# Expert masks spread over the partitions by TensorE instead of through DRAM, in a decoder layer on one core

## The chip, the cores and the metric

One Trainium2 chip, one of its cores. The metric is the device time of one execution of the whole kernel in microseconds; lower is better. TensorE (PE) multiplies into PSUM, VectorE (DVE), ScalarE (ACT) and GpSimd (POOL) do the rest, SyncE (SP) issues every transfer.

## The reference

Four batches of 512 rows with 128 features, three residual blocks behind a layer norm each. The third is the one that the change is about:

```python
x = x + attn(layernorm(x), gamma)                # scores are minus squared distances of the rows
x = x + xattn(layernorm(x), ctx, ctx, ...)       # 16 heads of 8, 154 context rows, ALiBi slopes
# x = x + ffn(layernorm(x), ...), with h the normed rows:
logits = einsum('bsh,eh->bse', h, router_w) + router_b
_, top = top_k(softmax(logits), 2)
mask = one_hot(top, 8).sum(-2)                   # 1 for each of a row's two experts, else 0
out = einsum('bse,ehd,bsd->bsh', mask, expert_w, h) + einsum('bse,eh->bsh', mask, expert_b)
```

Every expert is computed for every row, with the rows that did not choose it set to zero.

## The kernel before, in words

Each engine has a list of steps (`ORDER`), walked strictly in that order; `walk` (L110) calls a step as `steps[name](b, k)`, with `b` the batch and `k` a part of it. Semaphores between steps do the rest, so an engine whose next step has to wait holds up all its later steps. Batches overlap: while PE and ACT do the cross attention of one batch, the self attention and the queries of a later one are woven in. `WARM` gives, for some steps, a number of idle matmuls (`warm`, L825, recorded at L828) that PE does ahead of the step's wait, into a bank that nobody needs; they keep PE busy.

PSUM has eight banks. `ST` (two) holds attention scores. `MX` (two) holds the score groups whose row maxima DVE takes; batch `b` fills it 22 times (two groups in each of eleven `maxima` steps), in turn into the two banks, and the semaphores `a_ps` and `maxed` count filled and reduced groups. `MX[0]` also takes the transposed maxima (`mT`). `YV` takes the values' products, the output projection (`wo`), the router's logits and the experts' sum. `YM` takes transposes of `pvs`, `ao`, `y3`, of the masks and of the result `fT`. `A0` and `A1` serve the self attention and the queries.

What a batch passes through, with the lines used below:

- Self attention (`dist`, `soft`, `probs`, `self`), then `y2T` and `query`. DVE's `query` (L725 to L729) splits the queries into three bf16 parts; SP writes the parts to `q_scratch` and reads them back stacked into `qs`, which the maxima's matmuls (L928) need.
- `maxima` (PE L928, DVE L736), `mcat`, `mT`; SP carries `mT` through `m_scratch` into `qs`.
- `scores` (PE L952 and L957, exponentials ACT L584) in twelve parts, and `values` (PE L974 and L976), a part for each quarter of the heads. `values` of a batch's first part waits for `fT_sb`, as the experts of the batch before sat in the same bank `YV`.
- `divide` (transposes of `pvs`, DVE L757 and L759), `aoT`, `wo` (L996), third layer norm `y3`, its transpose `y3T`.
- `route`: PE L1009 multiplies `y3T` with the router's weights, DVE ranks the logits in seven instructions (L782 to L797) and leaves a bf16 mask. `mask`: PE transposes it (L833), ACT copies it to `maskT16`, whose first eight partitions are the eight experts' rows of 512 ones and zeros.
- The row of an expert has to lie on all 128 partitions before it can be multiplied with `y3T`. SP's `mask` writes the eight rows to `e_scratch` in DRAM and, when these have landed, reads them back in two transfers that repeat each row over 128 partitions, into `mask_all`.
- `select`: DVE (L807, experts 0, 2, 4, 6) and POOL (L504, experts 1, 3, 5, 7) multiply `mask_all` with `y3T` into `ym`, one instruction of 128x512 for each expert. Step `select` is one item of the list of either engine, so its four instructions are not parted.
- `experts` (PE): one bias matmul (L1025) and eight fp32 matmuls (L1028, two recorded instructions each), adding up in `YV`. It is one item of PE's list too.
- `fT` (ACT copy, PE transposes), `store` (DVE L813 adds the residual, SP stores).

In PE's list `experts:0` stands ahead of `dist:3`, `experts:1` ahead of `values:2.0`, `experts:2` ahead of `values:3.0`, and `experts:3` is last but one.

Of the kernel before, what the change touches and what calls it, by code (L numbers as in the profile page):

```python
# [15 lines left out]
E = 8
P = 128
# [42 lines left out]
        soft:3.1 scores:1.7 scores:1.8 scores:1.9 scores:1.10 scores:1.11 probs:3.0 values:1.1 soft:3.2  # L60
        values:1.3 soft:3.3 aoT:1 probs:3.1 probs:3.2 probs:3.3 mT:2 y3T:1 mask:1 scores:2.0 scores:2.1 y2T:3
        scores:2.2 scores:2.3 scores:2.4 scores:2.5 query:3 fT:1 scores:2.6 values:2.1 scores:2.7 scores:2.8
        scores:2.9 scores:2.10 scores:2.11 values:2.3 aoT:2 y3T:2 mT:3 mask:2 scores:3.0 scores:3.1 scores:3.2
        scores:3.3 scores:3.4 fT:2 scores:3.5 scores:3.6 scores:3.7 scores:3.8 scores:3.9 scores:3.10
# [7 lines left out]
        divide:0.1 maxima:1.9 maxima:1.10 mcat:1 wo:0 y3:0 gather:2 route:0 y2:2 y1:3 query:2 select:0 dist:3
        rowmax:3 maxima:2.0 maxima:2.1 maxima:2.2 maxima:2.3 maxima:2.4 maxima:2.5 maxima:2.6 maxima:2.7 store:0
        divide:1.0 divide:1.1 maxima:2.8 maxima:2.9 wo:1 maxima:2.10 mcat:2 y3:1 gather:3 route:1 y2:3 select:1
        query:3 store:1 divide:2.0 maxima:3.0 maxima:3.1 maxima:3.2 maxima:3.3 maxima:3.4 maxima:3.5 divide:2.1
        maxima:3.6 maxima:3.7 wo:2 maxima:3.8 y3:2 maxima:3.9 maxima:3.10 mcat:3 route:2 select:2 store:2
# [1030 lines left out]
```

## Time and profile before

| | us |
|---|---|
| median of 3 runs | 294.41 |
| lowest and highest | 293.37 to 298.64 |
| profiled execution, its device time | 294.32 |
| its span in the trace | 292.2 |
| mean granted TensorE clock, 1 is 2.4 GHz | 0.951 |
| busy: PE, PEld (weight loads) | 232.6, 111.6 |
| busy: DVE, ACT, POOL | 162.9, 109.3, 62.0 |

The span runs from the first to the last instruction of the profiled execution; some 2.1 us of the device time lie around it. Busy times overlap between engines. PE's busy time holds the warm matmuls, and as matmuls are pipelined, the mean length of one (393 ns for 512 columns of bf16) is more than its share of PE: back to back ones start closer together.

### The profile page before, as it was taken

To read this page: it belongs to the slowest core of one execution; us is meant where nothing else is said; L and a number is where in the kernel's file an instruction comes from. 1 tells how busy PE (TensorE), PEld (TensorE's weight loads), DVE (VectorE), ACT (ScalarE), POOL (GpSimd) and SP (SyncE) were. 2 spreads that over 40 slices of the span, in tenths; PEclk is the share of its full clock that TensorE was granted. 3 is DMA by queue.
4 is the path that set the end of the run, shared out by engine and by line. 5 is a ranking of instruction groups with operands and counts; after the bars stand their busy time and mean duration, and the time that the engine had idled before them with its cause. 6 is when DMAs were issued, how large, how long until landed. Compare 5 with 4: busy or idle time off the path is not lost.

```text
span 292.2 us, 3460 instructions
## 1 busy us (share of the span) xinstructions
PE 232.6 (80%) x1182; PEld 111.6 (38%) x1198; DVE 162.9 (56%) x406; ACT 109.3 (37%) x200; POOL 62.0 (21%) x112
## 2 busy tenths in 40 slices
PE   6778669777997899869997897978867698867774
PEld 2427323245332447434332752422334232143331
DVE  3856644993542887965673892915775240034270
ACT  2346055322774263570574318144102615210000
POOL 5234350001512001334000040800010260001071
PEclk9979999999798899999999999999979999789599
DMA  6942239002062012075001024170100600000231
GB/s 182 267 119 53 52 109 192 19 1 47 3 168 48 0 36 47 1 251 110 0 1 34 2 48 142 58 161 2 34 2 15 213 3 0 3 0 0 55 126 36
DMA packets 23029, 19.28 MB, mean 66 GB/s; under 512 B 10644, under 2 KB 21260, under 8 KB 22924
## 3 DMA queue, kind: packets, MB, share of 16 engines
q1 hardware_dynamic: 23012, 19.07, 25.2%
q8 instruction: 9, 0.15, 0.2%
q14 instruction: 8, 0.07, 0.1%
HBM read 13.65 MB, written 5.41 MB: 65 GB/s over the span
## 4 chain that ended last, share of the span: by engine, by line
PE 46%; DVE 26%; ACT 10%; issue 6%; DMA 6%; POOL 3%; another core or an unknown queue 1%; SPq 0%; ACTq 0%; DVEq 0%; POOLq 0%
DVE nm L736 10%; PE bank L1028 10%; PE bank L833 6%; PE bank L976 5%; PE bank L974 5%; ACT pt L584 4%; PE bank L868 4%; PE bank L828 3%; PE bank L928 3%; PE bank L887 2%; PE bank L952 2%; DMA qs<-m_scratch 2%; DVE st L628 2%; PE bank L996 2%; DMA mask_all<-e_scratch 2%
## 5 line engine op out<-in xcount | busy, mean ns | idle before, releaser
L736 DVE TENSOR_REDUCE nm<-bank 128x3 f32<-128x462 f32 x88 | 49.3, 619 | 18.8 <-PE bank L928 18.7
L584 ACT ACTIVATE pt<-bank 128x512 f32<-128x512 f32 x80 | 44.1, 596 | 31.6 <-PE bank L952 20.2
L828 PE MATMUL bank<-idle 128*128 128x512 bf16 x147 | 42.9, 434 | 3.1 <-DVE idle L623 1.5
L928 PE MATMUL bank<-kA,qs 128*128 128x308 bf16 (+1 forms) x172 | 29.9, 270 | 9.3 <-DVE nm L736 8.4
L428 POOL TENSOR_SCALAR ve<-mv 128x4 f32<-128x4 f32 x12 | 2.3, 194 | 155.9 <-DVE mv L631 155.7
L504 POOL TENSOR_TENSOR ym<-mask_all,y3T 128x512 f32<-128x512 bf16 x16 | 25.1, 1596 | 43.8 <-DMA mask_all<-e_scratch 43.8
L807 DVE TENSOR_TENSOR ym<-mask_all,y3T 128x512 f32<-128x512 bf16 x16 | 22.6, 1469 | 20.6 <-DMA mask_all<-e_scratch 20.6
L1028 PE MATMUL bank<-ym,ewT 128*128 128x512 f32 x64 | 28.7, 601 | 1.7 <-DVE ym L807 1.7
L952 PE MATMUL bank<-qs,kB 128*128 128x512 bf16 x58 | 20.4, 393 | 9.6 <-ACT pt L584 6.8
L828 PEld LDWEIGHTS bank<-idle 128*128 128x128 bf16 x154 | 16.5, 111 | 23.6 <-issue 11.2
L928 PEld LDWEIGHTS bank<-kA,qs 128*128 128x128 bf16 x172 | 13.0, 100 | 28.4 <-DVE nm L736 21.9
L974 PE MATMUL bank<-pt,vm 128*32 128x512 f32 x128 | 17.9, 632 | 7.1 <-ACT pvs L514 5.0
L868 PE MATMUL bank<-y1Tg,y1T 128*128 128x512 f32 x32 | 17.8, 639 | 4.6 <-ACT w L530 3.8
L655 DVE TENSOR_REDUCE rm<-bank 128x1 f32<-128x512 f32 x16 | 11.0, 691 | 18.4 <-PE bank L869 15.2
L976 PE MATMUL bank<-pt,vt 128*128 128x512 f32 x32 | 19.3, 687 | 0.0
L1028 PEld LDWEIGHTS bank<-ym,ewT 128*128 128x128 f32 x64 | 11.7, 189 | 17.0 <-issue 6.6
L530 ACT ACTIVATE w<-bank,snsq,sgn 128x512 f32<-128x512 f32 x16 | 12.3, 777 | 15.3 <-DVE rm L655 15.3
L887 PE MATMUL bank<-y,pT 128*128 128x128 f32 x128 | 15.2, 277 | 0.0
L514 ACT ACTIVATE fT<-bank 128x512 f32<-128x512 f32 x4 | 2.4, 597 | 34.0 <-PE bank L1028 34.0
L952 PEld LDWEIGHTS bank<-qs,kB 128*128 128x128 bf16 x64 | 6.2, 100 | 22.8 <-ACT pt L584 16.7
L887 PEld LDWEIGHTS bank<-y,pT 128*128 128x128 f32 x128 | 14.6, 192 | 0.2
L638 DVE TENSOR_SCALAR y<-x,mv,rs 128x128 f32<-128x128 f32 x32 | 10.3, 382 | 6.4 <-POOL rs L430 6.4
(132 smaller groups left out, 281.2 us busy)
## 6 DMA issues: line engine op xcount, KB each, us to landing
mask_all<-e_scratch SPq DMA_DIRECT2D x8, 512.0 KB, 4.8
qs<-q_scratch SPq DMA_DIRECT2D x8, 384.0 KB, 5.3
q_scratch<-qpart SPq DMA_DIRECT2D x4, 384.0 KB, 2.5
xs<-in_x_dram SPq DMA_DIRECT2D x4, 256.0 KB, 7.1
q_scratch<-qpart SPq DMA_DIRECT2D x4, 256.0 KB, 2.2
out_dram<-ob SPq DMA_DIRECT2D x4, 256.0 KB, 5.7
kA<-k_scratch SPq DMA_DIRECT2D x8, 120.0 KB, 2.8
kB<-k_scratch SPq DMA_DIRECT2D x8, 120.0 KB, 2.5
```

The source lines that it names most:

```text
L504: g.tensor_tensor(ym[:, e, :], mask_all[:, e, :], y3T[:, :], ALU.mult).then_inc(masked_p, 1)
L584: nc.scalar.activation(pt[:, n % PT_RING, :], ST[n % 2][:, :], ACT.Exp).then_inc(exps, 1)
L736: v.tensor_reduce(negated[:, GROUP * g:GROUP * g + heads], MX[n % 2][:, 0:heads * J].rearrange("p (s j) -> p s j", s=heads), AX.X, ALU.max ...
L807: v.tensor_tensor(ym[:, e, :], mask_all[:, e, :], y3T[:, :], ALU.mult).then_inc(masked_v, 1)
L828: mm(bank_[:, :], idle[:, 0:P], idle[:, :], start=True, stop=True)
L868: mm((A0, A1)[t % 2][:, :], y1T[:, tile(t)], y1Tg[:, :], start=True, stop=False)
L887: last = mm(A0[:, tile(t)], pT[:, t, u, :], y1[:, u, :], start=(u == 0), stop=(u == T - 1))
L928: last = mm(MX[n % 2][:, at * J:(at + heads) * J], qs[:, b % 2, a, tile(t)], kA[:, s:s + heads, a, 0:J], start=True, stop=True)
L952: last = mm(ST[n % 2][:, :], kB[:, h % 2, h // 2, 0:JM], qs[:, b % 2, h // 2, :], start=True, stop=True)
L974: mm(YV[32 * g:32 * g + 32, :], vm[:, b, R * g + k, :], pt[:, (n + g) % PT_RING, :], start=(k % 2 == 0), stop=False, skip_group_check=True)
L976: mm(YV[:, :], vt[:, b, k, :], pt[:, (n + G) % PT_RING, :], start=False, stop=(k % 2 == 1), skip_group_check=True).then_inc(pv_ps, 1)
L1028: last = mm(YV[:, :], ewT[:, e, :], ym[:, e, :], start=False, stop=(e == E - 1))
```

## The change

The masks' round trip through DRAM goes, with SP's step `mask`, `e_scratch`, `mask_all` and their semaphores. A constant `spread` (128 partitions x 8 x 128, bf16, loaded at the start, ahead of the experts' weights) holds for expert `e` a matrix whose row `e` is ones. A new PE step `spread:b.e` multiplies it with `maskT16` into a bank of `MX`: the expert's row on all partitions. DVE's `select:b.e` multiplies that bank with `y3T`; POOL's `select` is gone. `MX` is now filled by maxima and spreads in one common count (`mx_full`, `mx_free`), in this order of batches: maxima 0, maxima 1, spread 0, maxima 2, spread 1, maxima 3, spread 2, spread 3. `experts` and `select` are parted by expert, and each may stand anywhere in the lists. The experts' sum and the logits move from `YV` to `YM`, so `values` no longer waits for `fT_sb`. All five lists and `WARM` are new; of the lists the diff shows first three places of DVE's, then PE's around the masks of the four batches (what stood there before is told above).

```diff
-        keys:0 gather:0 y2:0 stats1:1 y1:1 query:0 dist:1 rowmax:1
+        keys:0 stats1:1 gather:0 y2:0 y1:1 query:0 dist:1 rowmax:1
...
-        wo:0 y3:0 gather:2 route:0 y2:2 y1:3 query:2 select:0 dist:3
+        wo:0 stats1:3 y3:0 gather:2 route:0 y2:2 select:0.0 select:0.1 y1:3
+        select:0.2 select:0.3 query:2 select:0.4 select:0.5 select:0.6 select:0.7 dist:3 maxima:2.0
...
-        maxima:2.10 mcat:2 y3:1 gather:3 route:1 y2:3 select:1
-        query:3 store:1 divide:2.0 maxima:3.0
+        maxima:2.10 mcat:2 y3:1 gather:3 route:1 y2:3 select:1.0 select:1.1
+        select:1.2 select:1.3 select:1.4 select:1.5 query:3 select:1.6 select:1.7 maxima:3.0
...
+        scores:1.1 scores:1.2 scores:1.3 values:1.0 mask:0 y2T:2 scores:1.4 spread:0.0 spread:0.1 query:2
+        experts:0.0 spread:0.2 spread:0.3 experts:0.1 spread:0.4 experts:0.2 experts:0.3 scores:1.5 spread:0.5
+        y1T:3 experts:0.4 experts:0.5 scores:1.6 spread:0.6 spread:0.7 dist:3 maxima:2.0 experts:0.6 scores:1.7
+        maxima:2.1 experts:0.7
...
+        route:1 scores:2.0 mask:1 scores:2.1 spread:1.0 spread:1.1 y2T:3 experts:1.0 spread:1.2 query:3
+        spread:1.3 spread:1.4 experts:1.1 spread:1.5 experts:1.2 experts:1.3 experts:1.4 scores:2.2 spread:1.6
+        experts:1.5 spread:1.7 scores:2.3 experts:1.6 scores:2.4 scores:2.5 values:2.0 scores:2.6 values:2.1
+        scores:2.7 maxima:3.0 experts:1.7 scores:2.8 maxima:3.1 scores:2.9 maxima:3.2 scores:2.10 fT:1
+        maxima:3.3 scores:2.11 values:2.2 maxima:3.4 values:2.3 maxima:3.5 divide:2.0
...
+        mT:3 route:2 mask:2 scores:3.0 spread:2.0
+        spread:2.1 scores:3.1 spread:2.2 spread:2.3 scores:3.2 experts:2.0 experts:2.1 scores:3.3 experts:2.2
+        spread:2.4 scores:3.4 experts:2.3 spread:2.5 scores:3.5 values:3.0 scores:3.6 experts:2.4 spread:2.6
+        scores:3.7 experts:2.5 scores:3.8 values:3.1 scores:3.9 spread:2.7 experts:2.6 scores:3.10 experts:2.7
+        scores:3.11 values:3.2 values:3.3 fT:2 divide:3.0 divide:3.1 aoT:3 wo:3 y3T:3 route:3 mask:3 spread:3.0
+        spread:3.1 experts:3.0 spread:3.2 experts:3.1 spread:3.3 spread:3.4 experts:3.2 spread:3.5 experts:3.3
+        experts:3.4 spread:3.6 spread:3.7 experts:3.5 experts:3.6 experts:3.7 fT:3
...
 WARM = {
-    "y1T:0": 16, "probs:0": 12, "y2T:0": 16, "query:0": 4, "y1T:1": 5, "maxima:0": 13, "scores:0": 3, "y2T:1": 1,
-    "divide:0.0": 1, "y3T:0": 2, "mask:0": 8, "y2T:2": 3, "route:1": 3, "mask:1": 11, "scores:2": 1, "y3T:2": 5,
-    "route:2": 1, "mask:2": 5, "scores:3": 9, "experts:2": 1, "wo:3": 1, "y3T:3": 13, "mask:3": 4,
-    "experts:3": 14, "fT:3": 2,
+    "y1T:0": 16, "probs:0": 10, "y2T:0": 16, "query:0": 4, "y1T:1": 4, "maxima:0": 14, "scores:0": 7, "y2T:1": 1,
+    "query:1": 2, "values:0.0": 2, "maxima:1": 1, "scores:1": 2, "y3T:1": 3, "scores:2": 6, "spread:1": 1,
+    "wo:2": 1, "y3T:2": 3, "scores:3": 1, "wo:3": 3, "y3T:3": 16, "mask:3": 7, "spread:3": 1,
 }
...
+        def maxima_fill(b, g):
+            return b * GROUPS + E * max(0, b - 1) + g
+        def spread_fill(b, e):
+            return min(b + 2, B) * GROUPS + E * b + e
...
+            load(spread[:, :, :], spread_rows, expert_in)
             load(ewT[:, :, :], expert_w, expert_in)
...
-            def mask(b, _):
-                sp.wait_ge(mask_sb, b + 1)
-                load(e_scratch, maskT16[0:E, :], e_out)
...
-                for i in range(2):
-                    half = slice(i * E // 2, (i + 1) * E // 2)
-                    load(mask_all[:, half, :], e_scratch[half, :].partition_broadcast(P), e_in[i])
...
-                    pe.wait_ge(fT_sb, b)
+                    pe.wait_ge(x2_ready, b)
...
+            def select(b, e):
+                if e == 0:
+                    dve.wait_ge(y3T_sb, b + 1)
+                    if b >= 1:
+                        dve.wait_ge(f_ps, b)
+                n = spread_fill(b, e)
+                dve.wait_ge(mx_full, n + 1)
+                v.tensor_tensor(ym[:, e, :], MX[n % 2][:, :], y3T[:, :], ALU.mult).then_inc(mx_free, 1)
...
+            def spread_(b, e):
+                n = spread_fill(b, e)
+                if e == 0:
+                    pe.wait_ge(mT_sb, min(b + 2, B))
+                    pe.wait_ge(mx_free, n)
+                    warm(MX[n % 2], f"spread:{b}")
+                    pe.wait_ge(mask_sb, b + 1)
...
+                pe.wait_ge(mx_free, n - 1)
+                mm(MX[n % 2][:, :], spread[:, e, :], maskT16[:, :], start=True, stop=True).then_inc(mx_full, 1)
+            def experts(b, e):
+                if e == 0:
+                    pe.wait_ge(mask_sb, b + 1)
...
+                    mm(YM[:, :], ebias[:, :], maskT16[:, :], start=True, stop=False)
+                pe.wait_ge(mx_free, spread_fill(b, e) + 1)
+                last = mm(YM[:, :], ewT[:, e, :], ym[:, e, :], start=False, stop=(e == E - 1))
+                if e == E - 1:
+                    last.then_inc(f_ps, 1)
```

## Rows read from the trace of the kernel before

**Rows 1.** The page's slices: granted TensorE clock in tenths, 40 slices of 7.3 us.
```profile
PEclk9979999999798899999999999999979999789599
```

**Rows 2.** Stretches: us, busy us of PE, PEld, DVE, ACT, POOL, clock, DMA share, GB/s.
```profile
0.00:117.09 117.09, 92.80 (x518) 48.00 (x525) 72.88 (x211) 50.49 (x93) 28.27 (x84) 0.96 0.35 84
...
117.09:137.39 20.30, 16.54 (x72) 7.86 (x74) 14.52 (x30) 9.48 (x17) 8.36 (x7) 1.00 0.48 130
...
170.93:200.57 29.64, 25.05 (x111) 9.93 (x111) 15.00 (x31) 12.06 (x22) 8.99 (x7) 1.00 0.35 93
...
200.57:226.84 26.27, 19.79 (x116) 10.04 (x117) 19.02 (x48) 5.75 (x10) 1.21 (x2) 0.94 0.06 14
...
226.84:255.84 29.00, 24.12 (x92) 7.56 (x95) 6.09 (x5) 11.93 (x22) 6.38 (x4) 0.94 0.17 55
...
272.06:292.20 20.14, 14.62 (x40) 5.91 (x41) 6.08 (x5) 1.19 (x2) 6.37 (x4) 0.84 0.27 79
```

**Rows 3.** The same stretches, warm matmuls (L828) alone: PE and PEld busy, clock, DMA.
```profile
117.09:137.39 20.30, 2.71 (x11) 0.95 (x11) 1.00 0.48 130
...
200.57:226.84 26.27, 5.65 (x19) 2.03 (x20) 0.94 0.06 14
```

**Rows 4.** Groups by form: busy us, mean ns; idle before, releaser.
```profile
L1028 PE MATMUL bank<-ym,ewT 128*128 128x512 f32 x64 | 28.7, 601 | 1.7 <-DVE ym L807 1.7
...
L504 POOL TENSOR_TENSOR ym<-mask_all,y3T 128x512 f32<-128x512 bf16 x16 | 25.1, 1596 | 43.8 <-DMA mask_all<-e_scratch 43.8
...
L807 DVE TENSOR_TENSOR ym<-mask_all,y3T 128x512 f32<-128x512 bf16 x16 | 22.6, 1469 | 20.6 <-DMA mask_all<-e_scratch 20.6
...
L813 DVE TENSOR_TENSOR ob<-bank,x 128x512 f32<-128x512 f32 x4 | 2.8, 689 | 18.5 <-PE bank L833 18.5
```

**Rows 5.** Waits of the maxima's matmuls: us in total, times, longest.
```profile
PE bank L928 <- DVE nm L736: 8.4, 31, 2.2
```

**Rows 6.** Chain that ended last, last batch from the masks' copy: start, us, what.
```profile
272.71 0.61 ACT maskT L514
...
273.33 1.30 DMA e_scratch<-maskT
...
274.71 4.47 DMA mask_all<-e_scratch
...
279.30 0.70 DVE ym L807
...
280.05 7.30 PE bank L1028 x16
...
287.38 0.60 ACT fT L514
```

**Rows 7.** Timeline, batch 1's masks to batch 3's first maxima: start, us, what, idle.
```profile
175.64 0.40 PE L833 MATMUL bank<-ident,maskp 128*128 128x128 bf16 x4 [0.63 <-DVE maskp L797]
...
192.25 0.85 SPq L311 DMA_DIRECT2D qs<-q_scratch  x2
...
200.57 0.56 PE L928 MATMUL bank<-kA,qs 128*128 128x308 bf16 x4
```

**Rows 8.** Timeline, first values matmuls at two clocks and their successors.
```profile
191.00 1.07 PE L974 MATMUL bank<-pt,vm 128*32 128x512 f32 x8 [0.69 <-ACT fT L514]
...
193.06 1.06 PE L974 MATMUL bank<-pt,vm 128*32 128x512 f32 x8
...
250.23 1.94 PE L974 MATMUL bank<-pt,vm 128*32 128x512 f32 x8 [1.19 <-ACT pvs L514]
```

**Rows 9.** Timeline, early: POOL before two norms, warm matmuls back to back.
```profile
32.82 0.20 POOL L428 TENSOR_SCALAR ve<-mv 128x4 f32<-128x4 f32 x1 [7.12 <-DVE mv L631]
...
37.34 0.19 POOL L428 TENSOR_SCALAR ve<-mv 128x4 f32<-128x4 f32 x1 [2.14 <-DVE mv L631]
...
48.56 2.97 PE L828 MATMUL bank<-idle 128*128 128x512 bf16 x13
```

**Rows 10.** The page's DMA issues: KB each, median us from issue to landing.
```profile
qs<-q_scratch SPq DMA_DIRECT2D x8, 384.0 KB, 5.3
```

More of the change, by code:

```diff
@@ L56 @@
+        query:0 y1T:1 dist:1 soft:1.0 soft:1.1 probs:1.0 soft:1.2 soft:1.3 probs:1.1 probs:1.2 probs:1.3 mT:0
         scores:0.0 scores:0.1 scores:0.2 scores:0.3 y2T:1 scores:0.4 query:1 scores:0.5 scores:0.6 y1T:2
-        scores:0.7 scores:0.8 dist:2 values:0.1 soft:2.0 scores:0.9 scores:0.10 scores:0.11 soft:2.1 soft:2.2
-        values:0.3 probs:2.0 soft:2.3 aoT:0 probs:2.1 probs:2.2 probs:2.3 mT:1 y3T:0 scores:1.0 scores:1.1
-        scores:1.2 mask:0 y2T:2 query:2 scores:1.3 scores:1.4 scores:1.5 y1T:3 fT:0 dist:3 scores:1.6 soft:3.0
@@ L60 @@
[L60 to L64, printed above, removed]
@@ L65 @@
-        scores:3.11 values:3.1 values:3.3 aoT:3 y3T:3 mask:3 fT:3
+        scores:0.7 scores:0.8 values:0.1 dist:2 soft:2.0 soft:2.1 soft:2.2 scores:0.9 scores:0.10 soft:2.3
+        scores:0.11 probs:2.0 probs:2.1 values:0.3 probs:2.2 probs:2.3 aoT:0 mT:1 y3T:0 scores:1.0 scores:1.1
+        scores:1.2 scores:1.3 mask:0 y2T:2 scores:1.4 query:2 scores:1.5 y1T:3 scores:1.6 dist:3 scores:1.7
+        scores:1.8 fT:0 soft:3.0 scores:1.9 scores:1.10 scores:1.11 soft:3.1 values:1.1 values:1.3 probs:3.0
@@ L66 @@
     """,
     "vector": """
-        stats1:0 y1:0 weights:0 dist:0 rowmax:0 keys:0 gather:0 y2:0 stats1:1 y1:1 query:0 dist:1 rowmax:1
+        stats1:0 y1:0 weights:0 dist:0 rowmax:0 keys:0 stats1:1 gather:0 y2:0 y1:1 query:0 dist:1 rowmax:1
         maxima:0.0 maxima:0.1 maxima:0.2 maxima:0.3 maxima:0.4 maxima:0.5 maxima:0.6 maxima:0.7 maxima:0.8
-        maxima:0.9 maxima:0.10 mcat:0 stats1:2 gather:1 y2:1 y1:2 query:1 stats1:3 dist:2 rowmax:2 maxima:1.0
-        maxima:1.1 maxima:1.2 maxima:1.3 maxima:1.4 maxima:1.5 maxima:1.6 maxima:1.7 divide:0.0 maxima:1.8
@@ L72 @@
[L72 to L76, printed above, removed]
@@ L77 @@
-        divide:3.0 divide:3.1 wo:3 y3:3 route:3 select:3 store:3
+        maxima:0.9 maxima:0.10 mcat:0 gather:1 y2:1 stats1:2 y1:2 query:1 dist:2 divide:0.0 rowmax:2 maxima:1.0
+        maxima:1.1 maxima:1.2 maxima:1.3 maxima:1.4 maxima:1.5 maxima:1.6 maxima:1.7 maxima:1.8 divide:0.1
+        maxima:1.9 maxima:1.10 mcat:1 wo:0 stats1:3 y3:0 gather:2 route:0 y2:2 select:0.0 select:0.1 y1:3
+        select:0.2 select:0.3 query:2 select:0.4 select:0.5 select:0.6 select:0.7 dist:3 maxima:2.0 maxima:2.1
@@ L83 @@
         scores:0.3 y2T:1 scores:0.4 query:1 scores:0.5 values:0.0 scores:0.6 y1T:2 scores:0.7 values:0.1
-        scores:0.8 dist:2 values:0.2 maxima:1.0 divide:0.0 maxima:1.1 scores:0.9 maxima:1.2 maxima:1.3
-        maxima:1.4 scores:0.10 maxima:1.5 probs:2.0 maxima:1.6 scores:0.11 maxima:1.7 values:0.3 maxima:1.8
-        probs:2.1 divide:0.1 probs:2.2 maxima:1.9 aoT:0 maxima:1.10 wo:0 probs:2.3 mT:1 self:2 y3T:0 scores:1.0
-        route:0 scores:1.1 scores:1.2 mask:0 y2T:2 query:2 scores:1.3 scores:1.4 y1T:3 scores:1.5 scores:1.6
@@ L88 @@
-        experts:0 dist:3 maxima:2.0 values:1.0 maxima:2.1 fT:0 scores:1.7 maxima:2.2 values:1.1 maxima:2.3
-        probs:3.0 scores:1.8 maxima:2.4 scores:1.9 maxima:2.5 scores:1.10 maxima:2.6 scores:1.11 values:1.2
-        maxima:2.7 values:1.3 divide:1.0 maxima:2.8 divide:1.1 probs:3.1 aoT:1 probs:3.2 maxima:2.9 wo:1
-        maxima:2.10 probs:3.3 self:3 mT:2 y3T:1 route:1 mask:1 scores:2.0 scores:2.1 y2T:3 scores:2.2 scores:2.3
-        scores:2.4 scores:2.5 query:3 scores:2.6 experts:1 values:2.0 values:2.1 scores:2.7 fT:1 divide:2.0
@@ L93 @@
[L93 to L97 removed]
+        scores:0.8 dist:2 divide:0.0 maxima:1.0 values:0.2 maxima:1.1 scores:0.9 maxima:1.2 maxima:1.3 probs:2.0
```

134 lines of the change are left out of this document (59 added, 75 removed).

## The prediction, made before the change was run

> **What bounds the kernel now.** I read the page's slices first, then busy time by stretch, the groups by form, the chain of waits, and the timeline where it led. No engine is full. The span is 292.2 us. PE comes nearest, but in the stretches from 117.09 on part of its time is warm matmuls: 2.71 of 16.54 us in the first and 5.65 of 19.79 us in the one from 200.57 [rows 2, 3]. So PE does real work in 13.8 of 20.3 us there, and in 14.1 of 26.3 us in the other. What fills the rest is order: PE's list is strict, and each batch comes to a point where masks must be spread before PE can go on. In the last batch nothing lies beside this. The masks are copied at 273.32, the first product starts only at 279.30, PE's expert block runs from 280.05 to 287.35, and the copy of the result starts at 287.38 [rows 6]: 14.06 us from masks to result copy, 5.98 of them transfers. In the other batches DVE and POOL wait for the same transfers (20.6 us over three waits on DVE, 43.8 on POOL [rows 4]). The clock bounds too: it is full in most slices, but 0.5 in the 38th [rows 1], and 0.84 to 0.94 in the late stretches [rows 2].
>
> **The change part by part.** Prices first.
>
> A product on DVE takes 0.70 us where it runs alone (the last batch's first, [rows 6]); over all 16 it is 1469 ns, and POOL's are 1596 ns [rows 4], because the two slow each other. The new one reads a PSUM bank and an SBUF tile as 128x512 fp32; the nearest row is the residual addition, 689 ns [rows 4]. I take 0.70. DVE then does eight in 5.6 us where it did four in 5.9 and POOL four in 6.4. Bounds: 0.69, and 1.47 if something still slowed them.
>
> A spread is a bf16 matmul of 512 columns, the form of a warm one: 13 take 2.97 us [rows 9]; with 0.38 us for the last to come through that is 0.216 apiece at full clock. 32 of them add 6.9 us of PE time. The expert block keeps its 7.30 us for 16 passes [rows 6], 0.91 an expert. The `WARM` tables hold 154 matmuls before and 121 after; 33 fewer are 7.1 us of filler, worth nothing by themselves as they sat in waits.
>
> *Tail (batch 3).* Masks ready at 273.32. First spread through at about 273.75, first product done at 274.45, first expert matmul at 274.5. Two spreads and the bias lie ahead of it; six more spreads lie inside. From there PE is the bound (0.91 + 0.22 an expert against 0.70 on DVE): 274.5 + 7.30 + 6 x 0.216 = 283.1, against 287.35: 4.25 us less. Before, 14 warm matmuls covered the wait for the transfers, and the 38th slice has the clock at half [rows 1]; now experts run in that time. Work worth 1.7 us less would be done if the half clock stayed to 277.6, where that slice ends (half of 274.1 to 277.6). I take half of that: **-3.4**, bounds -2.5 and -4.25.
>
> *Batch 2's masks (226.84 to 255.84, 29.00 us).* PE's real work here at full clock: 16 score matmuls 3.5, four tails at one such each 0.9, four `values` at 2.06 (start to start, [rows 8]) 8.2, experts 7.3, bias 0.2, spreads 1.7, transposes of `fT` 0.4 (fp32 columns at an expert's rate): 22.3. Before it was 20.5 in 29.0: scores and exponentials first, then the expert block in one piece while ACT stood still, then `values` at half clock once (1.94 us against 1.07 for the same eight [rows 8]). Now single experts lie between scores, so PE works while ACT does exponentials. ACT needs 11.9 [rows 2] and is no bound; the last exponentials and the copy of `pvs` stay exposed. I allow 2.2 of idle: 24.5, **-4.5**. Bounds: 0, and -6.7 with none.
>
> *Batch 1's masks to batch 3's maxima.* From the masks' transposes (175.64) to the first maxima of batch 3 (200.57) pass 24.9 us [rows 7]. Batch 3's queries came from DVE only behind its four slow products, so `qs` was asked for at 192.25, and PE had the expert block to finish. New order: scores 2.6, two `values` 4.1, seven experts and bias 6.6, spreads 1.7, `y2T` and `query` 1.3, masks 0.2: 16.6, and some 1.5 of waits give 18.1. The queries now stand behind six products. Masks copied by about 177.3, then on PE six spreads 1.3, two experts 1.8, `y2T` and `query` 1.3 and a wait or two: the sixth product ends near 183. Splitting the queries and writing them out I put at 4.4 (an estimate: three DVE instructions of at most 0.70 each, and a write no longer than half the 5.3 us of the read), so the request goes out near 187.4 and, at 5.3 us to landing [rows 10], is there by 192.7, in time for 193.7. That is 6.8 less. But one expert, `values` 2.2, a divide, transposes and a score part (4.3 us of PE) stood ahead of these maxima and now stand among them. DVE has 19.0 us to do in the 26.3 that follow and PE 14.1 [rows 2, 3], so I let half of it come back, with the spread work 2.3: **-4.5**, bounds 0 and -6.8.
>
> *Batch 0's masks (117.09 to 137.39, 20.3 us).* PE's real work was 13.8. It gains spreads 1.7 and `values:1.0` 2.06, and loses two experts, 1.8: 15.8. With 1.5 of waits it is 17.3: **-3.0**. The later work balances (a `values` less, two experts more). Bounds 0 and -4.5.
>
> *Start.* `stats1:1` moves ahead of `gather:0`, into DVE's idle time. POOL began that norm at 37.34 and had begun the one before at 32.82 [rows 9]; it can follow at 35.2, 2.1 earlier. Behind it come `y1T:1` and `dist:1`, but then maxima wait for `qs`, whose transfer doesn't move. I take **-1.0**, bounds 0 and -2.1. The extra load of 256 KB stands ahead of the experts' weights, for which POOL waits; POOL is then idle for 7.12 us before 32.82 [rows 9], which hides it. It would show only beyond that. SP loses its mask step, twelve transfers in all, so `query` is no longer behind a mask step; nothing is added there.
>
> The logits and experts in `YM`: `divide` waited for `YM` to be stored already, so this costs nothing, while `values` is freed from the experts. The remaining warm and order edits I set at nothing, within the bounds. The experts' new waits on DVE are the risk; they are the second and fourth rivals.
>
> Sum: 3.4 + 4.5 + 4.5 + 3.0 + 1.0 = 16.4. The profiled execution took 294.32 us (2.1 around its span), so 277.9; its time is 0.09 below the median of the runs, so **278.0 us**.
>
> A page speaks against this change. The Trainium skill, "TensorE: Matmul & The Clock Gate", section "A second HAM failure mode: psum-queue depth-cycling", tells of a kernel that went round PSUM banks, with small gaps on PE between groups of matmuls, and whose clock kept dropping and recovering. The trace agrees only in part: the maxima cycle through the same two banks with 31 waits of 0.27 us [rows 5], and most slices that hold them stand at 9 tenths [rows 1]. By the page the first rival below would come true; by the rows it is the lesser case.
>
> **The rivals.**
>
> *The clock falls in each expert block.* Spreads and experts alternate over two banks with gaps, and 33 warm matmuls are gone. For: `values` at half clock at 250.23, behind a stretch in which PE waited on exponentials; ahead of `scores:3` one warm matmul stands where nine did. Against: the new blocks are denser. There the eight matmuls took 1.94 for 1.07; a whole `values` part of 2.06 loses 1.7 at that ratio, and I take that for a fall. Four are 6.7 us, of which 0.9 is in my tail: 294.4 - 16.4 + 5.8 = **283.8**.
>
> *Hand-offs.* PE waits for DVE before each expert as it does in the maxima, 8.4 / 31 = 0.27 us [rows 5]; 32 x 0.27 = 8.7, hence **286.7**. Against it: two banks let a spread run ahead, and a product is shorter than an expert.
>
> *Only the exposed ends gain.* The middle batches are held by maxima, exponentials and the queries' transfers, and PE's freed time there turns into waiting. Then 3.4 + 4.5 = 7.9 remain: **286.5**. For it: 19.0 us of DVE work in 26.3 [rows 2].
>
> *Slower.* The experts go one at a time: spread, product, expert, with the next spread not issued until the expert is through, because in strict lists DVE's product stands behind work that waits for PE (`select:0.4` behind `query:2`). Idle of PE for each is then a product and both hand-overs, 0.70 + 0.27 + 0.1 = 1.07, or 34 us in all: **312**. It decides from 16.4 / 32 = 0.51 us of PE idle ahead of each expert. Against it: 31 waits in the maxima averaged half of that, over the same two banks and engines.
>
> *Everything at its good bound.* 4.25 + 6.7 + 6.8 + 4.5 + 2.1 = 24.4: **270.0**.
>
> **How the numbers follow.** Forecast 0.50, clock 0.13, hand-offs 0.12, only ends 0.09, slower 0.05, all good 0.11. A measurement of this kernel can tell about 2% from no change, so the limits are 288.5 and 300.3. The forecast's own spread (half of the distance to each bound) is 272 to 284; the range must take in the three rivals near 284 to 287 and the good case, but can leave the slower one out: **268 to 288**. Faster: all but the slower case and some of the upper ends of the middle three, 0.88; within 2% 0.07; slower 0.05.
>
> **What would show it.** Right: the first product of batch 3 starts within 0.6 us of the end of the masks' copy; products average 0.70; PE's idle ahead of L1028's successors stays under 0.1 us an expert; the last expert block takes 8.6 us or, at half clock, up to 10.3; the first maxima of batch 3 start 9 to 12 us earlier than at 200.57; from the first scores of batch 3 to its divide 24.5 us. Wrong: products at 1.4 us; a wait of PE on DVE's products of 0.5 us or more each; a mean clock under 0.9; the maxima of batch 3 as late as now; or queries of batch 2 or 3 that land later, since the middle of the sum hangs on them.

## The result, and the profile after

The changed kernel takes 279.66 us (median of 4 runs, 278.62 to 282.18) beside 296.52 us for the kernel before on the same chip (293.37 to 299.08): a ratio of 0.953, 95% interval 0.942 to 0.964. The forecast was 278.0 us. Executions of one kernel differ here by 1 to 3% with the clock they are granted, so differences of a few us are read from several kernels, and the ratios here and below (a kernel's time over that of the kernel before on the same chip) compare only the runs within 1.5% of their kernel's fastest.

The page's slices of the changed kernel (slices of 6.9 us), which answer [rows 1]:

```profile
PEclk9979979999999999999999999999997799979599
```

The 5 still stands in the 38th slice. Stretches between ACT's copies that end each batch's maxima (`mT:0` to `mT:3`), then to the last masks' copy, then to the end of the last result's copy (columns as in [rows 2]). The kernel before:

```profile
65.31:111.87 46.56, 39.97 (x218) 19.48 (x221) 27.40 (x76) 24.76 (x47) 8.67 (x25) 0.93 0.20 47
111.87:170.10 58.23, 49.94 (x292) 27.52 (x294) 39.59 (x98) 26.68 (x50) 10.79 (x11) 1.00 0.23 59
170.10:222.03 51.93, 42.00 (x212) 19.20 (x217) 32.93 (x79) 17.22 (x31) 10.20 (x9) 0.97 0.23 60
222.03:272.71 50.68, 38.36 (x164) 15.47 (x167) 15.02 (x35) 14.91 (x28) 7.58 (x6) 0.91 0.10 34
272.71:287.98 15.27, 13.32 (x32) 4.94 (x31) 5.39 (x4) 1.19 (x2) 6.37 (x4) 0.84 0.29 86
```

The changed kernel:

```profile
67.11:109.87 42.76, 38.68 (x227) 18.83 (x227) 26.35 (x68) 24.92 (x46) 6.43 (x14) 1.00 0.21 52
109.87:163.71 53.84, 48.53 (x293) 27.66 (x294) 38.69 (x109) 26.64 (x49) 8.22 (x18) 1.00 0.17 41
163.71:212.47 48.76, 39.81 (x209) 18.18 (x208) 31.74 (x81) 17.31 (x31) 3.87 (x5) 0.97 0.23 56
212.47:261.44 48.97, 39.78 (x177) 18.00 (x177) 15.43 (x40) 15.03 (x28) 1.20 (x2) 0.88 0.03 8
261.44:272.65 11.21, 10.28 (x26) 3.77 (x25) 5.25 (x8) 1.19 (x2) 0.00 (x0) 0.91 0.00 0
```

`mT:0` comes 1.8 us later (67.11 against 65.31). Then the stretches are 3.8, 4.4, 3.2, 1.7 and 4.1 us shorter: 17.1 in all, 15.3 net, against spans of 292.2 and 276.9. PE's busy time falls by 6.5 us (183.6 to 177.1 over these five), its idle time by 10.6 (39.1 to 28.5). The first 3.8 lie ahead of any mask: batch 0's masks are copied only in the second stretch.

Groups by form, which answer [rows 4]:

```profile
L1033 PE MATMUL bank<-ym,ewT 128*128 128x512 f32 x64 | 31.6, 596 | 0.0
L802 DVE TENSOR_TENSOR ym<-bank,y3T 128x512 f32<-128x512 f32 x32 | 21.1, 688 | 25.6 <-PE bank L1023 25.5
...
L1023 PE MATMUL bank<-maskT,spread 128*128 128x512 bf16 x32 | 11.6, 412 | 0.5 <-ACT maskT L510 0.3 <-DVE ym L802 0.2
```

The 32 products average 0.69 us, and the experts' matmuls have no idle time ahead of them. The tail's timeline, which answers [rows 6]:

```profile
261.44 0.60 ACT L510 ACTIVATE maskT<-bank 128x512 bf16<-128x512 bf16 x1 [5.14 <-PE bank L828]
262.09 1.04 PE L1023 MATMUL bank<-maskT,spread 128*128 128x512 bf16 x2 [0.26 <-ACT maskT L510]
262.84 1.29 DVE L802 TENSOR_TENSOR ym<-bank,y3T 128x512 f32<-128x512 f32 x2 [2.22 <-PE bank L1023]
263.58 1.13 PE L1033 MATMUL bank<-ym,ewT 128*128 128x512 f32 x2
...
272.05 0.60 ACT L510 ACTIVATE fT<-bank 128x512 f32<-128x512 f32 x1 [10.01 <-PE bank L1033]
```

From the masks' copy to the first product 0.80 us pass where 5.98 did (copy's end to product's start in both), to the result's copy 10.0 where 14.06 did. Batch 1's masks to batch 3's maxima, which answers [rows 7]:

```profile
169.63 0.40 PE L828 MATMUL bank<-ident,maskp 128*128 128x128 bf16 x4 [0.22 <-DVE maskp L791]
...
180.68 0.83 SPq L325 DMA_DIRECT2D qs<-q_scratch  x2
...
187.40 0.56 PE L923 MATMUL bank<-kA,qs 128*128 128x308 bf16 x4
...
187.79 0.64 DVE L730 TENSOR_REDUCE nm<-bank 128x3 f32<-128x462 f32 x1 [6.93 <-PE bank L923]
```

17.8 us where 24.9 passed. DVE now waits 6.93 us for these maxima: PE, no longer DVE's products and the queries, decides there.

### The profile page after: what moved, and what is told of

It is laid out like the page before. It is cut to its first block, busy times and chain, and to the rows that moved or that the text cites. A ratio compares the mean times of both kernels' runs of the same rounds, so it can differ in the third digit from the quotient of the medians.

```text
span 276.9 us, 3461 instructions
## 1 busy us (share of the span) xinstructions
PE 228.8 (83%) x1197; PEld 112.0 (40%) x1197; DVE 159.5 (58%) x422; ACT 109.5 (40%) x200; POOL 37.4 (13%) x96
## 4 chain that ended last, share of the span: by engine, by line
PE 59%; DVE 24%; ACT 6%; issue 6%; POOL 2%; DMA 1%; POOLq 0%; SPq 0%; DVEq 0%; ACTq 0%
PE bank L1033 10%; DVE nm L730 10%; PE bank L828 6%; PE bank L971 6%; PE bank L969 6%; PE bank L823 5%; PE bank L863 4%; PE bank L947 4%; PE bank L882 4%; PE bank L923 3%; PE bank L1023 3%; DVE y L632 2%; PE bank L1002 2%; ACT w L534 2%; PE bank L895 2%
## 5 line engine op out<-in xcount | busy, mean ns | idle before, releaser
L823 PE MATMUL bank<-idle 128*128 128x512 bf16 x121 | 36.5, 444 | 2.4 <-DVE idle L617 1.5
L802 DVE TENSOR_TENSOR ym<-bank,y3T 128x512 f32<-128x512 f32 x32 | 21.1, 688 | 25.6 <-PE bank L1023 25.5
L923 PE MATMUL bank<-kA,qs 128*128 128x308 bf16 (+1 forms) x172 | 28.5, 264 | 8.1 <-DVE nm L730 7.4
L1033 PE MATMUL bank<-ym,ewT 128*128 128x512 f32 x64 | 31.6, 596 | 0.0
L969 PE MATMUL bank<-pt,vm 128*32 128x512 f32 x128 | 16.9, 602 | 4.8 <-ACT pvs L510 4.8
L823 PEld LDWEIGHTS bank<-idle 128*128 128x128 bf16 x121 | 13.0, 112 | 19.2 <-issue 9.0
L649 DVE TENSOR_REDUCE rm<-bank 128x1 f32<-128x512 f32 x16 | 11.0, 691 | 16.8 <-PE bank L864 16.7
L971 PE MATMUL bank<-pt,vt 128*128 128x512 f32 x32 | 18.0, 645 | 0.0
L882 PE MATMUL bank<-y,pT 128*128 128x128 f32 x128 | 15.3, 278 | 0.0
L1033 PEld LDWEIGHTS bank<-ym,ewT 128*128 128x128 f32 x64 | 11.7, 190 | 7.5 <-DVE ym L802 3.7
L510 ACT ACTIVATE pT<-bank 128x512 f32<-128x512 f32 x16 | 9.1, 594 | 12.2 <-PE bank L828 12.2
L632 DVE TENSOR_SCALAR y<-x,mv,rs 128x128 f32<-128x128 f32 x32 | 10.3, 382 | 4.8 <-POOL rs L434 4.8
L534 ACT ACTIVATE w<-w,nrb,sgn 128x512 f32<-128x512 f32 x16 | 12.9, 805 | 0.3 <-DVE nrb L661 0.3
L434 POOL TENSOR_TENSOR rs<-ve,minus_half 128x4 f32<-128x4 f32 x12 | 12.5, 1042 | 1.0
```

The lines of the kernel that those rows point to most:

```text
L534: nc.scalar.activation(w[:, t, :], w[:, t, :], ACT.Exp, bias=nrb[:, t:t + 1], scale=sgn[:, :], accum_out=den[:, t:t + 1]).then_inc(p_ready, 1)
L802: v.tensor_tensor(ym[:, e, :], MX[n % 2][:, :], y3T[:, :], ALU.mult).then_inc(mx_free, 1)
L823: mm(bank_[:, :], idle[:, 0:P], idle[:, :], start=True, stop=True)
L882: last = mm(A0[:, tile(t)], pT[:, t, u, :], y1[:, u, :], start=(u == 0), stop=(u == T - 1))
L923: last = mm(MX[n % 2][:, at * J:(at + heads) * J], qs[:, b % 2, a, tile(t)], kA[:, s:s + heads, a, 0:J], start=True, stop=True)
L969: mm(YV[32 * g:32 * g + 32, :], vm[:, b, R * g + k, :], pt[:, (n + g) % PT_RING, :], start=(k % 2 == 0), stop=False, skip_group_check=True)
```

## The experiments

**Taking the transport away, in the old lists.** In e1_old_no_transfers and e9_old_no_transfers_clean one part is left out: the masks don't reach the products, which multiply by constants. e1 filled them by a POOL memset:

```diff
+                done(g.memset(mask_all[:, :, :], 1.0))
 def mask(b, _):                      # sync
-    load(e_scratch, maskT16[0:E, :], e_out) ... load(mask_all...)
+    pass
 def select(b, _):                    # vector, gpsimd
-        pool.wait_ge(e_in[e // (E // 2)], ONE * (b + 1))
+    pool.wait_ge(mask_sb, b + 1)
```

> The old kernel with the masks' transfers taken out: no write to e_scratch, no read back, mask_all set to ones once by POOL at the start, and the products of DVE and POOL wait for the masks' copy on ACT instead. So the product uses ones instead of the masks; everything else, the lists too, is the old kernel's. If the round trip is the whole of what the change saved, this saves at least as much as the change (ratio 0.953 or below, some 14 to 17 us). My theory: the gain is made of the round trip where it is exposed, and of parting the expert block so that it lies beside scores; then this gives about 6 us in the tail and up to 5 in each earlier batch where DVE or PE stood before the transfers, some 9 to 13 us in all, 0.955 to 0.97. If the transfers were hidden everywhere but in the tail, 6 us, 0.98. Products stay at 1.5 to 1.65 us.

294.48 us (10 runs) beside 295.73 (13 runs), less gain than any of the three expectations. `mT:0` came 4.3 us late, to which the memset (3.5 us at 18.8) may have added, and 14 warm matmuls still stood ahead of the last experts, so the total settles little; but the three stretches from `mT:1` to the last masks' copy (bounds as in the tables above) are 58.18, 50.59 and 50.31 us against 58.23, 51.93 and 50.68, so hardly shorter. e9 fills the constants by two early DMAs and takes those warm matmuls out (and the one ahead of `experts:2`):

```diff
-    "experts:3": 14, "fT:3": 2,
+    "experts:3": 1,
```

> The kernel before without the masks' transfers, cleaner than e1_old_no_transfers: the products still run at their 1.47 and 1.60 us on DVE and POOL, but they read constants laid in once at the start by two DMAs (so the mask's transport is left out, nothing else), and wait only for the masks' copy; the fourteen matmuls that kept PE busy ahead of the last experts are out. If transfers and products' waits were what the change removed in the middle, the time falls by 8 us or more, to 288 or under, and the first maxima of batch 3 start 5 us earlier or more. If the middle's gain is the weaving's, only the tail gains: the copy of the masks to the last copy takes 12 to 12.7 us against 14.7, the middle moves by under 2 us, and the time falls by 2 to 4 us.

291.27 us, ratio 0.986 (0.976 to 0.995). Its stretches:

```profile
68.41:114.70 46.29, 38.99 (x218) 19.25 (x221) 27.09 (x74) 24.72 (x47) 8.71 (x25) 0.96 0.20 48
114.70:173.84 59.14, 51.35 (x292) 27.89 (x294) 38.83 (x98) 26.70 (x50) 9.83 (x11) 0.97 0.15 40
173.84:225.40 51.56, 41.81 (x212) 19.07 (x217) 32.05 (x79) 17.22 (x32) 10.21 (x9) 0.97 0.16 40
225.40:275.51 50.11, 37.85 (x163) 15.39 (x165) 15.03 (x35) 14.91 (x27) 7.59 (x6) 0.91 0.06 18
275.51:286.45 10.94, 9.77 (x18) 3.71 (x17) 5.39 (x4) 1.19 (x2) 6.38 (x4) 0.78 0.00 1
```

The four stretches up to the last masks' copy sum to 207.1 us against 207.4 before: nothing. The last is 4.3 shorter (copy to copy 10.3 us, where 12 to 12.7 was expected): the tail's gain is the transfers', and it is all they cost in the old order. The products averaged 1227 ns on DVE and 1520 on POOL here, less than the 1469 and 1596 that were to be kept, which makes the missing gain of the middle no smaller.

**The experts in one piece again, with the broadcast.** e3_new_blocks gathers each batch's spreads and experts in PE's list, all else as changed:

```diff
-  scores:1.4 spread:0.0 spread:0.1 query:2 experts:0.0 ... scores:1.5 ... experts:0.7 maxima:2.2
+  scores:1.4 query:2 spread:0.0 spread:0.1 experts:0.0 spread:0.2 ... experts:0.7 scores:1.5 ... maxima:2.2
```

> The new kernel with the spreads and experts of batches 0, 1 and 2 in one piece each on PE (spread two ahead, then expert, spread in turn), as the old expert block was: ahead of scores:1.5, of scores:2.2 and of values:3.0. Batch 3 is unchanged. My theory (experts between scores fill PE while ACT does exponentials) expects a loss of 2 to 3 us for each block, 5 to 9 in all: 284.5 to 288.5 us where the new kernel has 279.7. Its rival, that the round trip alone made the gain and the weaving none, expects the new kernel's time within 1.5 us.

299.74 us (median of 4): the profiled run took 293.35 us at a mean clock of 0.947, the others 299.22 to 300.41 at 0.925 to 0.926. Even by the profiled run, beside 293.7 for the kernel before on that chip (median of the runs that its ratios use), the whole gain of the change is gone, which is more than either expectation gave it. In its trace the middle stretches are 59.33, 52.95 and 54.93 us against 53.84, 48.76 and 48.97. ACT's longest waits in that kernel:

```profile
ACT pt L580 <- PE bank L947: 28.5, 13, 11.7
ACT pt L580 <- PE bank L952: 22.4, 9, 10.0
```

The exponentials starve for 10.0, 9.1 and 11.7 us behind the three blocks; the longest such wait in the changed kernel is 4.9. The kernel before, with the experts also in one piece, has the same wait under another name, as ACT's copy `fT` comes next behind each block:

```profile
137.59 0.60 ACT L514 ACTIVATE fT<-bank 128x512 f32<-128x512 f32 x1 [6.10 <-PE bank L1028]
...
190.35 0.60 ACT L514 ACTIVATE fT<-bank 128x512 f32<-128x512 f32 x1 [6.18 <-PE bank L1028]
...
239.82 0.60 ACT L514 ACTIVATE fT<-bank 128x512 f32<-128x512 f32 x1 [7.63 <-PE bank L1028]
```

There a block took PE 7.0 to 7.3 us; in e3 it took 9.9, 9.7 and 8.6, with the spreads inside it and up to 1.0 us of waits for DVE's products. So the broadcast alone doesn't carry the gain, and an expert block costs ACT about its own length wherever one was tried. The blocks of e3 also stand elsewhere than the old ones; what that adds isn't separated.

**The other corners.** e8_new_lists_dram: the new lists, the old transport.

```diff
-  n = spread_fill(b, e)
-  dve.wait_ge(mx_full, n + 1)
-  v.tensor_tensor(ym[:, e, :], MX[n % 2][:, :], y3T[:, :], ALU.mult)
+  dve.wait_ge(e_in[e // (E // 2)], ONE * (b + 1))
+  v.tensor_tensor(ym[:, e, :], mask_all[:, e, :], y3T[:, :], ALU.mult)   # odd e: the same on gpsimd
```

> The changed kernel with all its new lists (experts parted and woven among scores and maxima, the values freed early, experts on the other bank), but with the masks still sent through DRAM by SP and multiplied half by DVE, half by POOL as before. If the gain of the middle is the weaving's, and the broadcast by PE gives only the tail, this comes to the new time plus the tail's 4 us: 284 to 288 us, and the first maxima of batch 3 start at 187 to 189 us as in the changed kernel. If the freed products and transfers are what the middle needs, waits for the products come up between the woven experts and it is 290 us or over, the first maxima of batch 3 at 192 us or later.

303.46 us, ratio 1.029 (1.019 to 1.038). The first expectation is missed by 15 us; the second holds (the first maxima of batch 3 start at 207.08), though a loss against the kernel before was not named. Timeline of batch 0's masks:

```profile
125.54 0.60 ACT L527 ACTIVATE maskT<-bank 128x512 bf16<-128x512 bf16 x1 [1.68 <-PE bank L846]
...
132.31 0.69 DVE L820 TENSOR_TENSOR ym<-mask_all,y3T 128x512 f32<-128x512 bf16 x1 [7.51 <-DMA mask_all<-e_scratch]
...
133.06 3.78 PE L1041 MATMUL bank<-ym,ewT 128*128 128x512 f32 x4 [4.97 <-DVE ym L820]
...
138.11 1.98 PE L1041 MATMUL bank<-ym,ewT 128*128 128x512 f32 x4 [1.28 <-DVE ym L820]
...
140.47 0.60 ACT L597 ACTIVATE pt<-bank 128x512 f32<-128x512 f32 x1 [11.22 <-PE bank L970]
```

The first product starts 6.2 us behind the masks' copy, and the new order has PE at its first expert 4.97 us before that product is done. PE waits, its clock falls (two pairs of passes in 3.78 us), and since every list is strict ACT waits 11.22. In the stretches that hold the first three batches' masks the clock was 0.92, 0.88 and 0.82, so part of the loss is the clock's, behind such waits. The old order has the experts late, where the slow transport is in time for them.

e10_old_lists_broadcast: the lists before, the broadcast.

```diff
-  y3:0 gather:2 route:0 y2:2 y1:3 query:2 select:0 dist:3
+  y3:0 gather:2 route:0 y2:2 y1:3 query:2 select:0.0 select:0.1 ... select:0.7 dist:3
-  scores:1.5 scores:1.6 experts:0 dist:3
+  scores:1.5 scores:1.6 spread:0.0 spread:0.1 experts:0.0 ... experts:0.7 dist:3
```

> The broadcast by PE alone: the code of the changed kernel (products from the maxima's banks on DVE, no transfers, none on POOL) with the step lists of the kernel before, the experts of batches 0 to 2 in one piece where they stood there; only the last batch's spreads and experts alternate as in the changed kernel. With it the four corners are there: old lists with transfers (before), new lists with transfers (e8_new_lists_dram), old lists with the broadcast, new lists with it (the changed kernel). If broadcast and weaving pay only together, this gains the tail's 4 us at most and gives some back for 24 more matmuls of 0.2 to 0.4 us and for 16 more products of 0.69 us on DVE within the scores: 290 to 298 us. If the broadcast alone carries the gain, it is under 286 us.

301.37 us, ratio 1.021 (1.012 to 1.030), above both expectations. It isn't a clean corner: the new code has no place for the warm matmuls ahead of the masks of batches 0 to 2, and from the masks' copy to the result's the clock was 0.73:

```profile
120.94:141.94 21.00, 18.56 (x53) 7.59 (x52) 8.61 (x17) 6.72 (x13) 0.00 (x0) 0.73 0.30 76
```

How much of its loss is that clock can't be told from here. But neither it nor e3_new_blocks shows any gain of the broadcast outside the tail.

**The slower rival made to happen.** e4_new_one_at_a_time puts each spread directly ahead of its expert and makes it wait until the product before is done:

```diff
-  pe.wait_ge(mx_free, n - 1)
+  pe.wait_ge(mx_free, n)
```

> The new kernel with each spread directly ahead of its expert in PE's list, and made to wait until both MX banks are free: spread, product, expert, one after the other, 32 times. My prediction priced the idle of PE at 1.07 us each, 34 us in all, which would put it at 314 us, slower than the old kernel. The rival reading: PE was not the bound in the middle, so part of this idle is free and only half or less shows, 290 to 300 us.

328.56 us, ratio 1.120 (1.110 to 1.130), 49 us over the changed kernel:

```profile
292.23 2.08 PE L1033 MATMUL bank<-ym,ewT 128*128 128x512 f32 x2 [0.46 <-DVE ym L802]
294.09 0.63 PE L1023 MATMUL bank<-maskT,spread 128*128 128x512 bf16 x1
294.76 0.69 DVE L802 TENSOR_TENSOR ym<-bank,y3T 128x512 f32<-128x512 f32 x1 [2.59 <-PE bank L1023]
295.51 2.08 PE L1033 MATMUL bank<-ym,ewT 128*128 128x512 f32 x2 [0.79 <-DVE ym L802]
```

3.28 us an expert: 0.79 idle, and the passes at the lower of the clock's two levels, 1.2 GHz (2.08 us for two; 1.13 in the changed kernel's first pair). That is the last batch; with the same idle, the blocks of batches 0 and 1 ran at the higher level (granted clock 1.00 in their stretches, 0.50 in the last batch's):

```profile
124.77 1.13 PE L1033 MATMUL bank<-ym,ewT 128*128 128x512 f32 x2 [0.78 <-DVE ym L802]
...
184.04 1.12 PE L1033 MATMUL bank<-ym,ewT 128*128 128x512 f32 x2 [0.79 <-DVE ym L802]
```

The stretches of the four batches' experts are 10.2, 8.4, 11.8 and 16.7 us longer than in the changed kernel. The first two are near the 8.6 that eight times 1.07 gives; the clock is what the last one has on top. Both expectations are missed, 314 by 15 us.

**POOL beside the products.** e6_new_pool_beside gives POOL four 128x512 products of its own on SBUF tiles, once a batch's masks are copied.

```diff
+ def beside(b, _):
+     for i in range(4):
+         done(g.tensor_tensor(busy[:, i % 2, :], ewT[...], ewT[...], ALU.mult))
```

> The new kernel, and POOL multiplies two SBUF tiles of 128x512 fp32 four times behind the copy of each batch's masks, that is beside DVE's products; its result is used by nobody. If two engines slow each other whenever both read SBUF, the new products beside them go from 0.69 to 1.4 us or more, as the old ones did. If it takes two SBUF inputs on DVE (the old product had two, the new one has a PSUM bank and one SBUF tile), they stay at 0.69 and POOL's take less than 1.6.

284.4 us (one run):

```profile
L810 DVE TENSOR_TENSOR ym<-bank,y3T 128x512 f32<-128x512 f32 x32 | 21.0, 686 | 27.0 <-PE bank L1031 24.0 <-remote 3.0
L506 POOL TENSOR_TENSOR busy<-ewT 128x512 f32<-128x512 f32 x16 | 20.3, 1269 | 19.9 <-ACT maskT L518 18.8
```

DVE's products from a bank don't slow (0.69), as the second expectation has it, and POOL's take 1.27 us, not 1.60 (both their inputs are fp32 here, where one was bf16). Another instruction of DVE does slow: the four of the normalisation `y` ahead of batch 0's third product took 3.82 us beside POOL's products,

```profile
125.36 3.82 DVE L640 TENSOR_SCALAR y<-xs,mv,rs 128x128 f32<-128x128 f32 x4
```

where the same four take 1.11 in the changed kernel (at 123.59). The products behind them came late, PE waited 2.51 us, and the stretch from `mT:1` to `mT:2` is 59.6 us where it was 53.8.

**The edits that the prediction set at nothing, and the start.** e5_old_pvs_first moves one step of ACT's list in the kernel before, e2_old_early_stats one of DVE's:

```diff
-  scores:0.7 scores:0.8 dist:2 values:0.1 soft:2.0      # scalar, e5
+  scores:0.7 scores:0.8 values:0.1 dist:2 soft:2.0
-  keys:0 gather:0 y2:0 stats1:1 y1:1                    # vector, e2
+  keys:0 stats1:1 gather:0 y2:0 y1:1
```

> The kernel before with one step of ACT's list moved: values:0.1 ahead of dist:2 instead of behind it. In the kernel before PE waits 2.08 us at 91.7 us for that copy and the clock then falls to half at 93 to 97.5 us; the new order of the change takes this wait away among its many small moves. If that wait is what the change gained between the first and the second mT copy, this one edit makes that stretch 2 to 4 us shorter (46.6 to about 43 or 44) and all later milestones with it; if it was something else there, under 1 us.

292.19 us, ratio 0.990 (0.983 to 0.997). What it removes, in the timeline of the kernel before, and the stretch in e5:

```profile
91.73 1.06 PE L974 MATMUL bank<-pt,vm 128*32 128x512 f32 x8 [2.08 <-ACT pvs L514]
92.72 1.66 PE L976 MATMUL bank<-pt,vt 128*128 128x512 f32 x2
94.17 0.97 PE L928 MATMUL bank<-kA,qs 128*128 128x308 bf16 x4
```

```profile
65.61:107.98 42.37, 37.09 (x218) 18.12 (x221) 27.36 (x76) 24.71 (x46) 8.71 (x25) 1.00 0.21 52
```

42.4 us against 46.6. In four other kernels with the old ACT order the stretch took 44.5 to 46.3, in the eight with the new one 42.8 to 43.6; so the edit is worth some 2 to 4 us in this stretch and 1% in all.

> The kernel before with one step of DVE's list moved: stats1:1 ahead of gather:0, as in the change. The prediction gave this 1.0 us less. The traces say the contrary: in the changed kernel the reciprocal of gather:0 waits behind those statistics, and x of batch 0 comes 1.1 us later. If that reading holds, y2T's first copy comes 0.5 to 1.2 us later than in the kernel before of the same chip and the time does not fall (0 to +1.5 us). If the prediction was right on its own and another edit made the start late, it falls by 1 us.

296.19 us (10 runs), ratio 1.002 (0.998 to 1.007): neither gain nor loss. The copy of `y2T:0` came at 35.85, against 36.80 before, earlier and not later, though that is inside what this copy shows between kernels with one and the same code up to it (36.05 to 37.92). In both DVE waits for PE's matmuls ahead of `x`, 2.48 and 3.47 us, which hides the statistics. My reading of the changed kernel's late start isn't borne out either.

**Improving on the change.** e7_new_fT_early, e11_new_fT_stats and e12_new_fT_stats_warm build on one another:

```diff
-  values:3.2 values:3.3 fT:2 divide:3.0         # tensor, all three
+  fT:2 values:3.2 values:3.3 divide:3.0
-  keys:0 stats1:1 gather:0 y2:0 y1:1            # vector, e11 and e12
+  keys:0 gather:0 y2:0 stats1:1 y1:1
-  "y3T:3": 16,                                  # e12
+  "y3T:3": 19,
```

> The changed kernel with one step of PE's list moved: the six transposes of batch 2's outputs (fT:2) go ahead of values:3.2 instead of behind values:3.3. PE waits 1.68 us there for the last exponentials' transposed copy, so the transposes fill a wait: 0.8 to 1.0 us less from the last scores to the divide. If the pairs behind them hang on PE's order alone and not on that wait, nothing changes or it is 0.5 us later.

> The kernel of e7_new_fT_early (fT:2 ahead of values:3.2) and stats1:1 put back behind y2:0 on DVE, as in the kernel before. If the early statistics cost the start what they seem to, x of batch 0 is 0.8 to 1.2 us earlier, the first milestones with it, and the time 275 to 276.5 us, the best so far. If the copies of y1T of batch 1, which then wait longer for their statistics, end the start instead, it is the time of e7_new_fT_early, 277.

> The kernel of e11_new_fT_stats with 19 instead of 16 matmuls on idle data ahead of the last y3T transposes: the changed kernel ran at half clock from 256.5 to 263.8 us, right behind a gap of 1.24 us in which PE had nothing. If the shorter gap keeps the clock up, the route's matmuls take 1.0 instead of 1.6 us and the spreads and first experts their full speed: 1 to 1.5 us less than e11_new_fT_stats. If the clock falls anyway, or the 19 run at half clock themselves, no less or up to 2 us more.

277.02, 278.34 and 279.22 us, ratios 0.940 (0.930 to 0.949), 0.943 (0.936 to 0.950), 0.945 (0.935 to 0.955). The stretch that `fT:2` lies in, from `mT:3` to the last masks' copy, in e7:

```profile
216.45:262.73 46.28, 38.09 (x174) 16.11 (x177) 15.52 (x40) 15.03 (x28) 1.20 (x2) 0.89 0.03 8
```

It is 46.3, 46.2 and 46.3 us in the three against 49.0 in the changed kernel and 49.1 in e6: 2.7 less. 1.2 us lie ahead of the copy `aoT:3` (34.0 us behind `mT:3`, not 35.2), where 0.8 to 1.0 was expected. The other 1.5 go with the clock: the transposes of `ao`, `wo:3` and the router's matmuls take 1.12, 1.59 and 1.62 us in the changed kernel, at half clock, and 0.66, 1.16 and 1.06 in e7. Why the clock stays up there isn't shown. The ratio's interval overlaps the change's, so the gain over it, about 1%, rests on that stretch. The statistics and three more warm matmuls add nothing, so the first expectation of each is missed and its second holds within the runs' spread: in e11 the router's matmuls (1.06 us) and the spreads already ran at full clock, which e12 wanted for them.

## Why the prediction was right, point by point

The total holds (16.9 us less in the medians, 16.4 forecast), and both of its main mechanisms: masks ready at once, and experts parted among other work. Its terms were less good than its sum, and that the sum came within half a us is luck: the two parts that it had wrong by 2.8 each (batch 2's masks, the start) are largely made up by 3.8 in a stretch that it put at nothing.

- *Tail, -3.4:* -4.1 (15.27 to 11.21; 14.67 to 10.6 to the copy's start). The block follows PE as worked out; e9's -4.3 shows that it is the transfers' price.
- *Batch 0's masks, -3.0, and batch 1's, -4.5:* the stretches that hold them came out 4.4 and 3.2 shorter. For batch 1 the working is visible: maxima of batch 3 began 23.7 us behind `mT:2`, not 30.5, so 6.8 less as forecast; 3.6 were given back by `mT:3`, where I had put 2.3.
- *Batch 2's masks, -4.5:* mis-sized. First scores to divide took 26.2 us, 2.8 less, and 1.1 came back in the rest of that stretch at half clock. The term had 24.5 us, PE's work with 2.2 of idle. The wait for the last `pvs` (1.68 us) and, behind `fT:2`, that for the store's addition (0.79) stood exposed; e7 fills part of the first.
- *Start, -1.0:* wrong. "Into DVE's idle time" was right, and POOL began that norm 3.0 us earlier in e2 (34.32, not 37.34), but nothing waited for it (e2: 1.002). The changed kernel's `mT:0` was 1.8 late; 67.11 lies among the 65.3 to 68.2 that `mT:0` showed in the four kernels whose code is the same up to there (the changed one, e3, e4, e7), so I don't put it down to an edit.
- *"Remaining order edits at nothing":* wrong by about 3. `values:0.1` ahead of `dist:2` alone is a ratio of 0.990, and the 3.8 us of the first stretch are mostly this move: they have nothing to do with masks or experts. What the rewritten `WARM` table adds was not tried by itself.
- *Products at 0.70:* 0.69. *Spreads at 0.216:* at full clock, yes; those in gaps or at the lower level run longer (0.41 us apiece in the records).
- *Rivals.* "Clock falls" did not come: the four stretches stand at 1.00, 1.00, 0.97 and 0.88, against 0.93, 1.00, 0.97 and 0.91 before. "Hand-offs": 0.0 us ahead of L1033 in the groups. "Only the exposed ends gain" is refuted by the stretches, but is exactly what e9, the transport's removal alone, does. "One at a time" is real when forced, and dearer than its 34: 49 us. Its price fits the two blocks that kept the full clock (10.2 and 8.4 us for 8.6) and left out the half clock, which the whole last block had.
- *What would show it:* products 0.69; last block 8.4 us (8.6 to 10.3); maxima of batch 3 at 187.40, 13.2 earlier (9 to 12); first product 0.80 behind the copy (0.6 was wanted; the spread ran at the lower clock).

What the prediction did not see is how the parts depend on each other. It added up edits; the four corners don't add:

| ratio to the kernel before | masks through DRAM | masks at once |
|---|---|---|
| experts in one piece | 1 (before) | 0.986 (e9, transport left out), 1.00 (e3, its 293.35 us alone), 1.021 (e10) |
| experts woven, early | 1.029 (e8) | 0.953 (the change) |

The order alone costs 3%, the broadcast with the experts in one piece gains nothing beyond the tail (in e3's trace the middle three stretches are 6.4 us longer than before; spreads inside PE's blocks and 16 more products on DVE are what it adds there), and both give 17 us. The move of `values:0.1`, 3 of these 17, is in e3, e8 and the change alike and needs neither. How much of e10's loss is its missing warm matmuls stays open, as does how much of e8's is the clock, and whether lists written for the slow transport, woven but later, could keep a part of the gain.

## What to carry to other kernels

Where lists are strict, a result that comes sooner is worth what can be moved up to it: reprice and rewrite the order with each change of latency, and test the two together, since either alone may show nothing or a loss. Part a long block of one engine (here 16 passes, 7.3 us) among the steps that feed the others; look at what the others wait for behind it, not at whether the engine is busy in it. A short wait early in a strict list (here 2.08 us for one copy) cost its length and then some 4 us in which the clock averaged 0.62, so such a wait is worth a small move of the step ahead of it.
